# A graph network on one core: gathers ahead of the bulk loads, sort tables in PSUM, twenty tiles written by rows with eighteen norms on GpSimd, and the other tiles' norms earlier in the loop

## Chip, core and metric

One Trainium2 chip, one of its cores. The metric is the device time of one launch in microseconds. The kernel before takes 2309.72 us, the median of three runs (2306.32 to 2310.63).

## What is computed

A graph has 6250 nodes with 16 features and 200000 edges with 16 features each; the edges are sorted by target node `dst`. A learned edge network gives each edge two 16 x 16 matrices (`W_attn`, `W_msg`, with biases); both are multiplied by the source node's features, a softmax over all edges of a target weighs the second by the first, and the sums are added to the node. After a layer norm the mean of the node's edge features is added, and a second layer norm follows:

```python
w_m = (efeat @ W_msg + b_msg).reshape(E, in_f, -1)
w_a = (efeat @ W_attn + b_attn).reshape(E, in_f, -1)
h_src = feat[src][:, :, None]
e1, e2 = w_m * h_src, w_a * h_src
ex = jnp.exp(e2 - segment_max(e2, dst)[dst])
attn = ex / segment_sum(ex, dst)[dst]
ft = segment_sum(e1 * attn, dst).sum(axis=1)
x = layernorm(x + ft)
x = layernorm(x + segment_sum(edge_attr, dst) / max(count, 1))
```

## The kernel before

**Tiles.** Nodes are sorted by degree, on the chip, into NC = 49 tiles of 128 nodes, one node per partition; tile k gets `CAPS[k]` edge slots (56 to 22, falling; 1628 in all), padded to an even number. A slot of a tile is one gather of 128 rows of `xt` by GpSimd (`gather`, L624). Slots go in groups of 8 or 6, and a group is the unit of a step of the loop; there are 224 groups and 240 steps and a few to drain.

**Head (common part).** SP loads constants and then the edge features `ea` in four parts of 3.1 MB (`features`, L458). GpSimd gathers one block of `dst` for each partition (L612), VectorE counts in it where the partition's nodes begin (L1201), GpSimd loads a window of `dst` (`WRUN`, L614) and the first tile's edge rows (L617), then gathers the first 48 slots. VectorE and ScalarE count the window (L1219, L801), which gives each node's degree. VectorE makes a histogram table `OH` of 26 bins x 48 nodes, its running sum `CUM`, ranks, and one-hot tables (`onehot`, L1259) in three sets; TensorE multiplies them (L1007) to permute the nodes. Beside this runs a check that the values stay in a safe range: ScalarE squares `ea` (`squares`, L787; it reads 16 floats apart), TensorE sums them (L993), VectorE takes maxima (L1274), TensorE transposes them (L1003), and VectorE computes `TOT` (L1281 to L1286). All engines wait for `TOT` in `fork` (L405) and take the `regular` branch here. GpSimd then waits for `v_tab`, VectorE's copy of the permuted edge starts `E0I` (L1292), which its next edge-row load needs (`runs_of`, L642).

**Loop.** Per step, TensorE transposes a group of edge features (`T`, L1023), multiplies it by the weights (`W`, L1034, into two pairs of PSUM banks), and adds up the slots of an older group (`gsum`, L1048, 2 matmul records for a slot). VectorE limits the gathered features of a tile once all have landed (`floors`, L1334), multiplies and takes the maximum (`mult`, L1348), multiplies exponentials (`gm`, L1361), and closes a tile (`weigh`, L1378 to L1380). ScalarE moves transposes out of PSUM (L819) and takes the exponentials (L881, L883, L887). The order on each engine is written out by hand from the list `STEPS`. The products lie in a ring of `RING = 66` slots in SBUF, the gathered features in one of 112 slots. After the gathers of tile k GpSimd scatters the result of tile k - 5 to `y_d` in node order (`results`, L657).

**End.** `MAIN = NC - 3 = 46` tiles go through `y_d`: when all have landed (and three scatters of zeros, L678, for the others' rows) SP loads `xt` and `y_d` in node order (L480, L481), VectorE does both layer norms for all 49 x 128 nodes at once, in four pieces `norms(0)` to `norms(3)` (L1402) at steps 235 to 238, and SP writes `out`. The last three tiles have their own `xt` rows gathered (L675); VectorE normalizes them by `last` (L1430, two tiles, then one, with ScalarE's square root at L835), and GpSimd scatters them straight into `out` (L685) after SP's write.

Of the kernel before, what the change touches and what calls it, by code (L numbers as in the profile page):

```python
# [54 lines left out]
MAIN = NC - 3  # L55
# [31 lines left out]
RING = 66  # L87
# [50 lines left out]
NST = len(STEPS) + 4  # L138


def gnn_kernel(nc, xt, dst, src, ea, es, wc, cst, cst2, out):
# [14 lines left out]
    with ctx:  # L156
# [9 lines left out]
        def arena(lowest=0):  # L166
# [50 lines left out]
        DGC = prep([128, RK1])  # L217
        PK = prep([128, RK1])
# [147 lines left out]
        RCL = sb("RCL", [128, 4])  # L366
# [4 lines left out]
        PMB = PX[:, 0, :]  # L371
        PDN = PX[:, 1:3, :].rearrange("p b e -> p (b e)")
# [9 lines left out]
            g_m g_b d_sc d_x a_sq p_sq p_c p_v v_nrm a_x a_p a_out d_y d_yl d_xg v_ys d_ou""".split()  # L382
# [67 lines left out]
        def _(sp):  # L450
# [7 lines left out]
            def features(q):  # L458
                n = min(QE, EC - QE * q)
                sp.dma_start(EAL[:, q % 2, 0:16 * n], ea.rearrange("(p c) w -> p (c w)", p=128)[:, 16 * QE * q:16 * QE * q + 16 * n])\  # L460
                  .then_inc(d_ea[q % 2], 16)

            features(0)
            sp.wait_ge(d_xe[0], 16)
# [13 lines left out]
            def regular():  # L478
                sp.wait_ge(S["d_y"], 16 * NC)
# [8 lines left out]
                sp.wait_ge(S["d_ou"], 48)  # L488
# [107 lines left out]
        def _(g):  # L596
# [11 lines left out]
            g.memset(RAW[:, :], 0.0).then_inc(S["g_m"], 1)  # L608

# [3 lines left out]
            g.wait_ge(S["v_e0"], 1)  # L613
# [17 lines left out]
            def regular():  # L631
# [1214 lines left out]
```

## Time and profile before

| | |
|---|---|
| median of 3 runs | 2309.72 us |
| profiled execution, its time | 2309.43 us |
| its span, first to last instruction | 2307.6 us |
| granted TensorE clock, mean | 0.946 |
| TensorE busy | 2005.4 us (87%) |
| VectorE busy | 1867.7 us (81%) |
| GpSimd busy | 1682.1 us (73%) |
| ScalarE busy | 1306.8 us (57%) |

PE is TensorE, DVE is VectorE, ACT is ScalarE, POOL is GpSimd, SP is the DMA-issuing engine. A line such as `L624` names the line of the kernel; all times are us unless marked ns. An "issue" wait is time in which the engine waited for nothing that the profile shows.

### The profile page before, as it was taken

To read this page: it belongs to the slowest core of one execution; us is meant where nothing else is said; L and a number is where in the kernel's file an instruction comes from. 1 tells how busy PE (TensorE), PEld (TensorE's weight loads), DVE (VectorE), ACT (ScalarE), POOL (GpSimd) and SP (SyncE) were. 2 spreads that over 40 slices of the span, in tenths; PEclk is the share of its full clock that TensorE was granted. 3 is DMA by queue.
4 is the path that set the end of the run, shared out by engine and by line. 5 is a ranking of instruction groups with operands and counts; after the bars stand their busy time and mean duration, and the time that the engine had idled before them with its cause. 6 is when DMAs were issued, how large, how long until landed. Compare 5 with 4: busy or idle time off the path is not lost.

```text
span 2307.6 us, 21909 instructions
## 1 busy us (share of the span) xinstructions
PE 2005.4 (87%) x6784; PEld 911.8 (40%) x6784; DVE 1867.7 (81%) x2922; ACT 1306.8 (57%) x1241; POOL 1682.1 (73%) x1748
## 2 busy tenths in 40 slices
PE   2548889998999998899989898899989898998886
PEld 0313334443444444444444443344444443444432
DVE  5557777987888988888987887798878887888886
ACT  6425545655566556665655755565556565565552
POOL 5777777777777777777777777777777777777740
PEclk8758999999999999999999999999999999999998
DMA  6100011001100001000100110101001010110110
GB/s 232 55 13 13 13 15 19 7 13 18 13 12 13 13 13 17 12 12 13 17 12 12 17 12 12 17 12 16 12 12 16 12 15 12 15 15 11 14 27 9
DMA packets 60072, 46.93 MB, mean 20 GB/s; under 512 B 28526, under 2 KB 55679, under 8 KB 59436
## 3 DMA queue, kind: packets, MB, share of 16 engines
q0 software_dynamic: 57776, 29.87, 9.3%
q1 hardware_dynamic: 2172, 15.58, 1.9%
q8 instruction: 57, 0.93, 0.2%
q14 instruction: 67, 0.55, 0.1%
HBM read 44.01 MB, written 1.23 MB: 20 GB/s over the span
## 4 chain that ended last, share of the span: by engine, by line
PE 36%; POOL 30%; issue 14%; DVE 14%; DMA 2%; ACT 2%; POOLq 0%; DVEq 0%; SPq 0%; ACTq 0%
POOL AR L624 29%; PE PX L1048 28%; PE PW L1034 7%; DVE AR L1348 7%; DVE AR L1361 3%; PE PTB L1023 2%; DVE AR L1378 1%; DMA AR<-in_xt,AR 1%; POOL AR L642 1%; DVE AR L1365 1%; POOL y_d L657 1%; DMA AR<-in_dst,QI 1%; ACT PX L881 0%; DVE AR L1379 0%; DMA AR<-in_es,AR 0%
## 5 line engine op out<-in xcount | busy, mean ns | idle before, releaser
L624 POOL DMA_INDIRECT AR<-in_xt,AR x1628 | 1572.2, 966 | 501.0 <-issue 486.6
L1048 PE MATMUL PX<-AR,CS 128*128 128x512 f32 x3304 | 1583.4, 604 | 6.8 <-ACT AR L825 6.6
L1348 DVE CUSTOM_DVE_ANT_1 AR<-PW,AR 128x1024 f32<-128x1024 f32 x826 | 987.7, 1220 | 183.0 <-PE PW L1034 127.6
L1048 PEld LDWEIGHTS PX<-AR,CS 128*128 128x128 f32 x3304 | 633.7, 193 | 586.5 <-issue 462.6
L1034 PE MATMUL PW<-WS,LT 100*128 100x512 bf16 x1652 | 514.8, 398 | 204.0 <-DVE AR L1348 203.0
L1361 DVE TENSOR_TENSOR AR<-AR,PX 128x1024 f32<-128x1024 f32 (+1 forms) x448 | 508.2, 1134 | 74.3 <-ACT PX L881 47.7
L819 ACT ACTIVATE LT<-PTB 100x1024 bf16<-100x1024 bf16 (+1 forms) x224 | 214.3, 957 | 529.8 <-PE PTB L1023 529.8
L883 ACT ACTIVATE AR<-AR 128x2048 f32<-128x2048 f32 (+1 forms) x224 | 429.3, 1917 | 7.3
L887 ACT ACTIVATE PX<-AR 128x1024 f32<-128x1024 f32 (+1 forms) x224 | 217.2, 970 | 326.4 <-DVE AR L1361 323.6
L1034 PEld LDWEIGHTS PW<-WS,LT 100*128 100x128 bf16 x1652 | 144.9, 99 | 584.2 <-issue 290.0
L881 ACT ACTIVATE PX<-AR 128x1024 f32<-128x1024 f32 (+1 forms) x224 | 235.6, 1052 | 22.9 <-DVE AR L1361 21.3
L1023 PEld LDWEIGHTS PTB<-IDB,AR 128*100 128x100 bf16 x1652 | 126.3, 128 | 132.6 <-issue 118.2
L1023 PE MATMUL PTB<-IDB,AR 128*100 128x128 bf16 x1652 | 132.8, 223 | 13.5 <-POOL AR L662 12.2
L1334 DVE TENSOR_TENSOR AR<-AR 128x128 f32<-128x128 f32 (+13 forms) x68 | 37.4, 563 | 113.6 <-DMA AR<-in_xt,AR 113.1
L1378 DVE RECIPROCAL AR<-AR 128x256 f32<-128x256 f32 x49 | 85.5, 1745 | 0.1
L1348 DVE DVE_READ_ACCUMULATOR2_ANT AR<- 128x1 f32 x826 | 68.4, 83 | 0.0
L825 ACT ACTIVATE AR<-PX 128x512 f32<-128x512 f32 x49 | 29.1, 594 | 52.2 <-PE PX L1048 52.2
L657 POOL DMA_INDIRECT y_d<-AR x46 | 45.0, 977 | 18.4 <-issue 13.4
L642 POOL DMA_INDIRECT AR<-in_es,AR x48 | 46.6, 971 | 14.6 <-issue 10.7
L851 ACT ACTIVATE AR<-AR 128x1088 bf16<-128x1088 bf16 (+13 forms) x49 | 55.6, 1134 | 0.0
L859 ACT ACTIVATE AR<-AR 128x1088 bf16<-128x1088 bf16 (+13 forms) x49 | 54.8, 1119 | 0.0
L1365 DVE TENSOR_REDUCE AR<-AR 128x16 f32<-128x544 f32 (+13 forms) x49 | 53.1, 1084 | 0.0
(149 smaller groups left out, 481.8 us busy)
## 6 DMA issues: line engine op xcount, KB each, us to landing
AR<-in_xt,AR POOLq DMA_INDIRECT x1631, 2.3
AR<-in_ea SPq DMA_DIRECT2D x3, 3128.0 KB, 13.6
AR<-in_ea SPq DMA_DIRECT2D x1, 3120.0 KB, 10.2
AR<-in_es,AR POOLq DMA_INDIRECT x49, 3.5
y_d<-AR POOLq DMA_INDIRECT x49, 2.1
AR<-y_d SPq DMA_DIRECT2D x1, 784.0 KB, 4.6
CS<-in_cst SPq DMA_DIRECT2D x1, 442.0 KB, 5.1
AR<-in_xt SPq DMA_DIRECT2D x1, 392.0 KB, 3.1
```

Of the source, the lines that this page charges most:

```text
L624: g.indirect_dma_start(feat(h, j - j0, j - j0 + 1), None, xt, bass.IndirectOffsetOnAxis(ap=XE[:, at:at + 1], axis=0)).then_inc(hg_sem(h), 16)
L819: a.activation(LT[:, g % 3, 0:128 * n], PTB[0:K, 0:128 * n], ACT.Copy).then_inc(S["a_T"], 1)
L881: a.activation(half(w), x[:, 0:w, :], ACT.Exp, bias=shift).then_inc(S["a_x"], 1)
L883: a.activation(x, x, ACT.Exp, bias=shift).then_inc(S["a_exp"], 1)
L887: a.activation(half(w), x[:, w:2 * w, :], ACT.Copy).then_inc(S["a_x"], 1)
L1023: i = pe.transpose(PTB[0:K, 128 * j:128 * j + 128], part(k, 0, K)[:, j0 + j, :], IDB[:, :])
L1034: i = pe.matmul(PAIRS[s % 2][:, j, :], LT[:, g % 3, lo:lo + 128], WS[:, :], start=True, stop=True)
L1048: i = pe.matmul(PDR, IDN, x, start=(a == 0 and j == 0), stop=(g == LAST[k] and j == n - 1))
L1348: v.tensor_tensor_reduce(em(g, j, j + 2).rearrange("p (x c) -> p x c", c=32), w, hb, 1.0, LOW, ALU.mult, ALU.max, accum_out=MXC[:, k % 2, ...
L1361: v.tensor_tensor(y, y, EXP[:, 0:16 * w].rearrange("p (x o) -> p x o", o=16), ALU.mult).then_inc(S["v_gm"], 1)
L1365: v.tensor_reduce(OUTR[:, k, 16:32], edge(k).rearrange("p j i -> p i j"), AX.X, ALU.add).then_inc(S["v_sa"], 1)
L1378: link(v.reciprocal(RRT, d[:, 0:256]))
```

## The change

1. **Loads.** SP holds `features(0)` until the first tile's edge rows are in; before it SP writes 784 KB of zeros over `y_d` (from `OUTR`, which GpSimd clears at the start), and `features(1)` waits for that write. GpSimd issues the edge rows before `WRUN`. `ea` is read from a transposed copy `eat` that holds each part with the 16 features outermost, so ScalarE's squares read adjacent floats; `squares(0)` comes after ScalarE's counts.
2. **Tables.** `OH`, `DGC`, `QFR`, `KF`, `PK`, a copy `FE1` of the edge starts, and `BASE` lie in PSUM (banks of `PW`), not in SBUF; the running sum takes a constant as its second input. The third one-hot set comes before the maxima. TensorE does the histogram first, then check(0) to check(2), the three permutation sets, check(3) and the transposes. VectorE, not GpSimd, sets the ones of `XP`.
3. **Tiles.** `MAIN` is 29: 20 tiles are written by rows. Of these, 18 get both norms on GpSimd after its last gather, in a batch of 16 and one of 2; the last 2 are normalized by VectorE and ScalarE (`last_batch`). GpSimd's norm has 26 instructions, each waiting for the one before, with a bit-trick root; the means take one more and each batch two additions: 109 in all. Each batch waits for its tiles' results (`a_out`), the first also for `v_ln`. The scatters of zeros and those of tiles 29 to 45 to `y_d` go; 17 more gathers of `xt` come, and 17 more scatters to `out`.
4. **Norms of the other 29 tiles**, still over all nodes at once: 14 pieces `main(0)` to `main(13)`, one a step, at steps 177 to 190 (during tiles 33 to 36).
5. **Last groups.** For the four groups consumed in the last steps without a product (`ADDS`: 218, 221, 222, 223) VectorE adds slots of the second half in pairs (`pairs`), and `gsum` takes 6, 6, 6 and 5 slots in place of 8, 8, 8 and 6.
6. `RING` is 64, which leaves the list of steps as it is; `YN` has its own place.

The diff, cut:

```diff
-MAIN = NC - 3
+MAIN = NC - 20
+REST = NC - MAIN
+BATCH = [(0, REST - 4), (REST - 4, REST - 2), (REST - 2, REST)]
-RING = 66
+RING = 64
+NORMS = [p for p, c in STEPS].index(FIRST[MAIN + 4] + 2)
+ADDS = [c for p, c in STEPS[-8:] if p is None]
...
+        OH = PWF[:, 512:512 + HB * RK1].rearrange("p (b c) -> p b c", c=RK1)
+        DGC, QFR, KF, PK, FE1 = (PWF[:, 1760 + RK1 * x:1760 + RK1 * x + RK1] for x in range(5))
+        BASE = PWF[:, 2000:2000 + HB]
...
+            sp.wait_ge(d_xe[0], 16)
+            sp.wait_ge(S["g_m"], 9)
+            sp.dma_start(YD.rearrange("(p c) w -> p c w", c=NC), OUTR[:, :, :]).then_inc(S["d_yz"], 16)
             features(0)
-            sp.wait_ge(d_xe[0], 16)
+            sp.wait_ge(S["d_yz"], 16)
             features(1)
...
             g.wait_ge(S["v_e0"], 1)
+            g.indirect_dma_start(XE[:, 0:17 * DEG[0]], None, es, bass.IndirectOffsetOnAxis(ap=R0[:, 0:1], axis=0)).then_inc(d_xe[0], 16)
+            g.wait_ge(S["v_e0"], 2)
             g.indirect_dma_start(WRUN[:, :], None, dst.unsqueeze(1), bass.IndirectOffsetOnAxis(ap=RI[:, 0:1], axis=0))\
              .then_inc(S["d_wr"], 16)
...
                 for k in range(1, NC):
                     feats(k)
-                    if k >= 5:
+                    if 5 <= k < MAIN + 5:
                         results(k - 5)
...
                 for k in range(MAIN, NC):
-                    g.indirect_dma_start(XG[:, k - MAIN, :], None, xt, bass.IndirectOffsetOnAxis(ap=NODE[:, k:k + 1], axis=0))\
+                    g.indirect_dma_start(YS[:, k - MAIN, :], None, xt, bass.IndirectOffsetOnAxis(ap=NODE[:, k:k + 1], axis=0))\
                      .then_inc(S["d_xg"], 16)
...
+                def norm(lo, hi):
+                    y, q = YS[:, lo:hi, :], SQS[:, lo:hi, :]
+                    s0, s1, s2 = STS[:, 0, lo:hi], STS[:, 1, lo:hi], STS[:, 2, lo:hi]
+
+                    def row_sums(z):
+                        then(g.tensor_tensor(q[:, :, 0:8], z[:, :, 0:8], z[:, :, 8:16], ALU.add))
+                        then(g.tensor_tensor(q[:, :, 0:4], q[:, :, 0:4], q[:, :, 4:8], ALU.add))
+                        then(g.tensor_tensor(q[:, :, 0:2], q[:, :, 0:2], q[:, :, 2:4], ALU.add))
+                        then(g.tensor_tensor(s0, q[:, :, 0], q[:, :, 1], ALU.add))
+
+                    row_sums(y)
+                    then(g.tensor_scalar(s0, s0, -1.0 / 16, None, ALU.mult))
+                    then(g.tensor_tensor(y, y, s0.unsqueeze(2).broadcast_to([128, hi - lo, 16]), ALU.add))
+                    then(g.tensor_tensor(q, y, y, ALU.mult))
+                    row_sums(q)
+                    then(g.tensor_scalar(s1, s0, 1.0 / 16, 1.0e-5, ALU.mult, ALU.add))
+                    then(g.tensor_scalar(SSI[:, 2, lo:hi], SSI[:, 1, lo:hi], -0.5, 1597463007.0, ALU.mult, ALU.add))
+                    for _ in range(3):
+                        then(g.tensor_tensor(s0, s2, s2, ALU.mult))
+                        then(g.tensor_tensor(s0, s0, s1, ALU.mult))
+                        then(g.tensor_scalar(s0, s0, -0.5, 1.5, ALU.mult, ALU.add))
+                        then(g.tensor_tensor(s2, s0, s2, ALU.mult))
+                    then(g.tensor_tensor(y, y, s2.unsqueeze(2).broadcast_to([128, hi - lo, 16]), ALU.mult))
...
+                g.wait_ge(S["v_ln"], 1)
+                means = OUTR[:, MAIN:NC - 2, 16:32]
+                then(g.tensor_tensor(means, means, RCL[:, 0:REST - 2].unsqueeze(2).broadcast_to([128, REST - 2, 16]), ALU.mult))
+                for b, (lo, hi) in enumerate(BATCH):
+                    if hi < REST:
+                        g.wait_ge(S["a_out"], MAIN + hi)
+                        then(g.tensor_tensor(YS[:, lo:hi, :], YS[:, lo:hi, :], OUTR[:, MAIN + lo:MAIN + hi, 0:16], ALU.add))
+                        norm(lo, hi)
+                        then(g.tensor_tensor(YS[:, lo:hi, :], YS[:, lo:hi, :], means[:, lo:hi, :], ALU.add))
+                        norm(lo, hi)
+                    else:
+                        g.wait_ge(S["v_ys"], 1)
+                    if b == 0:
+                        g.wait_ge(S["d_out"], 48)
+                    for x in range(lo, hi):
+                        g.indirect_dma_start(out, bass.IndirectOffsetOnAxis(ap=NODE[:, MAIN + x:MAIN + x + 1], axis=0), YS[:, x, :], None)\
+                         .then_inc(S["d_ou"], 16)
...
-                a.activation(SQ[:, q % 2, :, 0:n], EAL[:, q % 2, 0:16 * n].rearrange("p (e w) -> p w e", w=16), ACT.Square)\
+                a.activation(SQ[:, q % 2, :, 0:n], EAL[:, q % 2, 0:16 * n].rearrange("p (w e) -> p w e", w=16), ACT.Square)\
...
+            pe.wait_ge(S["v_hist"], 1)
+            pe.matmul(PMB[:, 0:HB], TRI, CNTB[:, :], start=True, stop=True)
+            pe.matmul(PMB[:, HB:2 * HB], ONES[:, :], CNTB[:, :], start=True, stop=True).then_inc(S["p_hist"], 1)
+            check(0)
+            pe.wait_ge(S["v_hist"], 2)
+            check(1)
+            check(2)
+            perm(0)
+            perm(1)
+            perm(2).then_inc(S["p_perm"], 1)
+            check(3)
+            pe.wait_ge(S["v_nrm"], 1)
...
+                def pairs(g):
+                    half = GRP[g][2] // 2
+                    keep = KEPT(half)
+                    v.wait_ge(S["a_exp"], g + 1)
+                    v.wait_ge(S["v_gm"], 2 * g + 2)
+                    sums = em(g, half, 2 * half - keep)
+                    v.tensor_tensor(sums, sums, em(g, half + keep, 2 * half), ALU.add).then_inc(S["v_ad"], 1)
...
-                    if 0 <= i - USED[LAST[MAIN]] - 2 < 4:
-                        norms(i - USED[LAST[MAIN]] - 2)
-                    if i - 3 == USED[LAST[NC - 2]]:
-                        last(0, 2)
-                last(2, 3)
+                    if 0 <= i - NORMS < 14:
+                        main(i - NORMS)
+                last_batch()
```

## Rows read from the trace of the kernel before

**Rows 1.** The page, part 1: busy time, share of the span, instructions.
```profile
PE 2005.4 (87%) x6784; PEld 911.8 (40%) x6784; DVE 1867.7 (81%) x2922; ACT 1306.8 (57%) x1241; POOL 1682.1 (73%) x1748
```
**Rows 2.** The page, part 5: group, busy us, mean ns, idle before and its releaser.
```profile
L624 POOL DMA_INDIRECT AR<-in_xt,AR x1628 | 1572.2, 966 | 501.0 <-issue 486.6
```
**Rows 3.** Who waited for whom: us in total, times, longest us.
```profile
DVE AR L1334 <- DMA AR<-in_xt,AR: 113.1, 27, 26.1
```
**Rows 4.** Timeline of VectorE, L1334: start us, us, instruction, idle before and releaser.
```profile
1132.43 0.72 DVE L1334 TENSOR_TENSOR AR<-AR 128x544 f32<-128x544 f32 x1 [2.31 <-DMA AR<-in_xt,AR]
...
1761.43 0.66 DVE L1334 TENSOR_TENSOR AR<-AR 128x480 f32<-128x480 f32 x1 [5.41 <-DMA AR<-in_xt,AR]
```
**Rows 5.** Busy time by stretch: stretch, its length, engines, clock, DMA share, GB/s.
```profile
1630.00:2230.00 600.00, 546.50 (x1845) 248.25 (x1844) 504.45 (x796) 352.28 (x356) 452.56 (x474) 0.97 0.10 13
```
**Rows 6.** Timeline of GpSimd in the head.
```profile
9.55 1.11 POOL L612 DMA_INDIRECT AR<-in_dst,QI  x1 [3.09 <-DVE QI L1196]
23.89 1.22 POOL L614 DMA_INDIRECT AR<-in_dst,AR  x1 [13.22 <-DVE AR L1204]
...
31.83 0.95 POOL L624 DMA_INDIRECT AR<-in_xt,AR  x1 [5.47 <-DMA AR<-in_es,AR]
...
45.58 2.02 POOL L624 DMA_INDIRECT AR<-in_xt,AR  x1 [0.30 <-issue]
...
102.96 0.95 POOL L642 DMA_INDIRECT AR<-in_es,AR  x1 [0.30 <-issue]
```
**Rows 7.** Timeline of VectorE in the head.
```profile
22.48 0.75 DVE L1201 TENSOR_SCALAR_CACHE_REDUCE AR<-AR,CS 128x512 f32<-128x512 f32 x1 [12.15 <-DMA AR<-in_dst,QI]
...
29.59 0.30 DVE L1219 TENSOR_SCALAR_CACHE_REDUCE AR<-AR,CS 128x88 f32<-128x88 f32 x1 [3.83 <-DMA AR<-in_dst,AR]
...
45.32 1.46 DVE L1227 TENSOR_TENSOR AR<-AR,CS 128x1248 f32<-128x1248 f32 x1
...
69.21 1.50 DVE L1274 TENSOR_REDUCE NRM<-PW 128x1 f32<-128x391 f32 x3
...
92.33 0.21 DVE L1292 CAST AR<-PX 128x49 int32<-128x49 f32 x1 [2.03 <-PE PX L1007]
```
**Rows 8.** DMA issues: what, engine, count, KB each, median us to landing.
```profile
AR<-in_xt,AR POOLq DMA_INDIRECT x1631, 2.3
AR<-in_ea SPq DMA_DIRECT2D x3, 3128.0 KB, 13.6
...
AR<-in_es,AR POOLq DMA_INDIRECT x49, 3.5
```
**Rows 9.** Timeline of ScalarE in the head.
```profile
13.90 0.87 ACT L786 ACTIVATE AR<-AR 125x800 f32<-125x800 f32 x1 [2.40 <-DMA AR<-in_xt]
22.29 10.73 ACT L792 ACTIVATE AR<-AR 128x6256 bf16<-128x6256 f32 x1 [7.52 <-DMA AR<-in_ea]
```
**Rows 10.** Groups by line: TensorE's permutation.
```profile
L1007 PE MATMUL PX<-AR 128*128 128x98 f32 x96 | 11.1, 276 | 0.0
```
**Rows 11.** Timeline of GpSimd in the tail.
```profile
2216.83 0.98 POOL L657 DMA_INDIRECT y_d<-AR  x1 [0.30 <-issue]
...
2295.51 0.96 POOL L685 DMA_INDIRECT out<-AR  x1 [3.85 <-DVE AR L1445]
```
**Rows 12.** Timeline of VectorE in the tail: a wide and a small operation.
```profile
2243.88 0.98 DVE L1408 TENSOR_TENSOR AR<-AR 128x784 f32<-128x784 f32 x1
...
2258.90 0.21 DVE L1395 TENSOR_TENSOR AR<-AR 128x49 f32<-128x49 f32 x1
```
**Rows 13.** Timeline of TensorE in the tail.
```profile
2249.20 0.60 PE L1034 MATMUL PW<-WS,LT 100*128 100x512 bf16 x2 [3.29 <-DVE AR L1348]
...
2267.04 19.26 PE L1048 MATMUL PX<-AR,CS 128*128 128x512 f32 x44 [1.73 <-ACT AR L825]
```
**Rows 14.** Timeline of GpSimd at the start.
```profile
0.74 0.51 POOL L597 MEMSET AR<- 1x512 bf16 x1 [0.29 <-POOLq L1836]
1.31 0.30 POOL L600 MEMSET AR<- 1x256 bf16 x1
```

More of the change, by code:

```diff
@@ L676, in regular @@
                      .then_inc(S["d_xg"], 16)
-                for k in range(MAIN, NC):
-                    g.indirect_dma_start(YD, bass.IndirectOffsetOnAxis(ap=NODE[:, k:k + 1], axis=0), OUTR[:, 0, :], None)\
-                     .then_inc(S["d_y"], 16)
-                for k in range(NC - 5, MAIN):
-                    results(k)
-                g.wait_ge(S["d_out"], 48)
-                for k in range(MAIN, NC):
-                    g.wait_ge(S["v_ys"], 1 if k < NC - 1 else 2)
-                    g.indirect_dma_start(out, bass.IndirectOffsetOnAxis(ap=NODE[:, k:k + 1], axis=0), YS[:, k - MAIN, :], None)\
-                     .then_inc(S["d_ou"], 16)
+                done = [0]
@@ new lines, in then @@
+                def then(i):
+                    done[0] += 1
+                    i.then_inc(S["g_b"], 1)
+                    g.wait_ge(S["g_b"], done[0])
+                def norm(lo, hi):
[19 more added lines that the diff above has]
+                    then(g.tensor_tensor(y, y, s2.unsqueeze(2).broadcast_to([128, hi - lo, 16]), ALU.mult))
@@ L808, in _ @@
             counts(0, len(BY_ACT))
+            squares(0)
             squares(1)
@@ L988, in _, with check @@
             pe.wait_ge(S["v_id"], 1)
-            for q in range(NQE):
+            def check(q):
                 n = min(QE, EC - QE * q)
@@ L1271, in _ @@
             onehot(*CUTS[1])
+            onehot(*CUTS[2])
             for q in range(NQE):
@@ L1408, in norms @@
                         link(v.tensor_tensor(XNN, XNN, YN[:, :, 0:16], ALU.add))
[L1409 to L1413 removed]
+                    if 1 <= x < 6:
+                        norm(x - 1)
+                    if x == 6:
+                        link(norm(5))
                         link(v.tensor_tensor(YN[:, :, 16:32], YN[:, :, 16:32], wide(RCG), ALU.mult))
+                    if x == 7:
@@ new lines, in added, with last_batch @@
+                def added(lo, hi):
+                    link(v.tensor_tensor(YS[:, lo:hi, :], YS[:, lo:hi, :], OUTR[:, MAIN + lo:MAIN + hi, 16:32], ALU.add))
+                def last_batch():
+                    lo, hi = BATCH[2]
+                    st = STS[:, :, lo:hi]
+                    for x in range(2):
+                        centre(lo, hi)
+                        spread(SQS[:, lo:hi, :], st).then_inc(S["v_var"], 1)
+                        v.wait_ge(S["a_z"], x + 1)
+                        link(v.reciprocal(STS[:, 0, lo:hi], STS[:, 2, lo:hi]))
+                        i = v.tensor_tensor(YS[:, lo:hi, :], YS[:, lo:hi, :], wide(STS[:, 0, lo:hi]), ALU.mult)
+                        if x == 0:
+                            link(i)
+                            added(lo, hi)
+                    i.then_inc(S["v_ys"], 1)
@@ L1465, in regular @@
                         gm(c, 1)
+                        if c in ADDS:
+                            pairs(c)
                     if nx is not None:
@@ L1802 @@
     eap = np.concatenate([ea, np.zeros((EP - E, 16), ea.dtype)])
+    eat = np.concatenate([eap.reshape(128, EC, 16)[:, lo:lo + EC // NQE + 1].transpose(0, 2, 1).reshape(128, -1)
+                          for lo in range(0, EC, EC // NQE + 1)], 1)
     srcp = np.concatenate([src, np.zeros(EP - E, src.dtype)])
```

211 lines of the change are left out of this document (96 added, 115 removed).

## The prediction

> **What bounds the kernel now.** I read the page first. GpSimd counts as busy for 73% of the span [rows 1], which looks harmless; the costliest groups show otherwise. The 1628 feature gathers of L624 take 0.966 us each, and in front of each stands 0.30 us of issue and nothing else [rows 2]. So GpSimd issues one DMA every 1.25 us, 1628 x 1.266 = 2061 us of a 2307.6 us span, with 48 loads of `in_es` and 46 scatters at the same price in the same queue. The only other place where the loop runs dry is VectorE waiting for gathered features, 113.1 us in 27 waits [rows 3]. In the timeline the longest, 26.1, stands before the first whole tile; then there is none until tile 20 at 1132 (2.31), and from there on almost each tile has one of 1 to 6 us, such as 5.41 at tile 35 [rows 4]. Thus GpSimd sets the start of the loop, TensorE and VectorE pace tiles 2 to 19 at nearly the same rate, and GpSimd sets the pace again from tile 20. There TensorE is busy 546.5 of 600 us and VectorE 504.5 [rows 5]: GpSimd may become some 5% faster before TensorE holds the loop.
>
> Three stretches are therefore worth money: the time to GpSimd's first gather, what stands in its queue, and the tail after its last gather.
>
> **Head: first gather.** The gather of `in_dst` by QI is issued at 9.55 and VectorE can use it only at 22.48, because the first 3.1 MB of `in_ea` were put in ahead of it [rows 6, 7]. In the change SP holds `features(0)` until the first edge rows are in. An indirect load of 487 KB lands in 3.5 us in the loop [rows 8]; this one is half as large, I take 3.3, so VectorE starts at 12.9, 9.6 earlier. The edge rows are then issued first, not second behind a slot of 1.5 us (1.22 + 0.30 at L614), at 14.4; with 3.5 us to land and 0.7 to start, the first L624 is at 18.6 instead of 31.83: 13.2 us. Bounds: 10 if the two loads take as long as before relative to each other, 14 at best.
>
> **Head: table stalls.** From 31.83 to L642 at 102.96 stand 48 gathers, 71.1 us where 48 x 1.25 = 60 would do. The 11.1 too many are in long issues such as 2.02 us at 45.58, beside VectorE's L1227 at 45.32 [rows 6, 7]. These are its tensor operations with both inputs in SBUF. The change puts one input of each (OH, QFR, KF, PK, FE1, BASE) into PSUM. The Trainium skill, "SBUF — State Buffer", section on the shared port pair, says that a VectorE instruction with two SBUF inputs contends with a GpSimd one that reads SBUF; the trace agrees so far. I take all 11.1; at worst nothing, but see what is late next. GpSimd would be at the fork (L642) at 18.6 + 60 = 78.6, and the two memsets of XP that leave its queue give 0.4.
>
> **Head: what is late next.** GpSimd goes on only when VectorE has copied E0I (L1292, 92.33) [rows 7]. Before, that was 10 us early; now it decides. The working: the long WRUN load lands about 22.5 (issued 15.7, 5.6 us before, more beside YD's zeroing, 0.8 MB, and `features(0)`). From the first count to the first L1274 VectorE took 69.21 - 29.59 = 39.6 us [rows 7], so with the third one-hot set it is done by about 67. The four squares: a load of `in_ea` takes 13.6 us [rows 8]. The first lands about 34, the second 44.5; the third can be issued only after `squares(0)`, and lands about 54.5. `squares` took 10.73 us for 6256 elements, 1.7 ns each, reading every 16th float, while L786 took 0.87 for 800, 1.1 ns with all its fixed time [rows 9]; with the transposed `eat` I take 5.9. Third squares done at 60.5, check(2) on PE to 65, then 48 permutation pairs, 11.1 us [rows 10], to 76. check(3), now behind them, ends at 80.5, for the maxima, the transposes and the verdict I put 3.5, for fork and copy 1.3 (these two, with the end of the permutation between them, are the last of the stretch to 92.33): E0I at 85.3. So GpSimd waits 6.7 us at the fork, and L642 moves from 102.96 to about 85.7. With the 0.4 of the memsets the **head gains 17.5 us**; the ends are 10.5 (E0I no earlier than now) and 24.8 (no wait). All consumers follow, since the first whole tile starts when its gathers land.
>
> **Loop.** Scatters to `y_d` cost 0.98 + 0.30 [rows 11]. Those of tiles 29 to 42, 14 of them, no longer stand before the last gather: -17.9. The two layer norms over all nodes go from the last steps to 177 to 190 (tiles 33 to 36). They are 13 wide operations of 1.01 us and 22 small of 0.24, with reciprocals 19.3 us [rows 12]. Per tile 4 to 6 us, what VectorE waits there (5.41 at tile 35 [rows 4]): I cost them at nothing on the end; without that cover up to 10 us. Their two-input forms will hold up some gathers: +3. SP's loads of XNN and YN wait for the result of tile 28 and have some 20 us until step 177. The other queues lose nothing.
>
> **Tail, TensorE and VectorE.** The norms no longer stand between the last multiplications. TensorE sat 3.3 us for VectorE at 2246 and 1.73 at 2265.3, and then did 22 slots in 19.26, 0.87 each [rows 13]. `pairs` adds slots of the last groups on VectorE, so 7 slots fall away: 6.1. Together 11.1. The last batch has two tiles for one, +0.3, and one more scatter, +1.25: this path ends 9.6 earlier, beside the head's gain.
>
> **Tail, GpSimd.** Today it idles there; now it won't. Without the head's gain: the slot after the last gather is at 2216.83 [rows 11], -17.9 + 3 = 2201.9. Twenty gathers of `xt`, 25.0, and landing 2.3 [rows 8]: 2229.2. Then 109 dependent small instructions over some 4200 elements per partition. No row shows such arithmetic on GpSimd. Lower bound 0.22, VectorE's small operation [rows 12]; upper bound 0.57, from the first memset to the one that waits for it (0.74 to 1.31); that second takes 0.30 by itself [rows 14]. I take 0.28, nearest the single memset, and VectorE's 1.25 ns per element: 109 x 0.28 + 5.3 = 35.8 (29 to 67). Sixteen scatters 20.3, two more 2.5, then the last two 1.6: the last one starts at 2289.4, against 2295.51 [rows 11]. So **the tail gains 6.1**, by GpSimd's chain, not by the 9.6 of the other path.
>
> The Trainium skill, "GPSIMD Engine Reference", section 3, speaks against this part: elementwise work on GpSimd is about 2x slower, 4497 ns for 2048 elements with two inputs. At that price an estimate for the 4200 elements is 9.2 us, not 5.3, and the tail would gain 2.
>
> **Sum.** 2309.43 (span 2307.6 and 1.8 around it, 0.3 below the median of the runs) - 17.5 - 6.1 = 2285.8.
>
> **Rivals.**
> A, the forecast: 0.45, between 2278 and 2296.
> B, full cover: E0I comes before 78.6, and GpSimd's norms cost 0.25 or less, so that the other path ends last: 2309.4 - 24.8 - 9.6 = 2275. For: VectorE has its tables at 67. Against: permutations wait behind the third squares. 0.2.
> C, slower: GpSimd's arithmetic is the new end. At 0.57 each the chain is 31.6 longer: 2285.8 + 31.6 = 2317. It decides from 0.49 each (23.6 / 109 more than 0.28). For: 109 instructions in series, each with a wait. Against: the memsets' own 0.3. 0.12.
> D, the head's new wait takes more: the loads of `in_ea` start 13 us later and all four are behind one another, so E0I stays at 92.5: 2309.4 - 10.5 - 6.1 = 2293. 0.13.
> E, the moved norms aren't hidden, since TensorE has only 9% left there: 10 us late at the last tile, the path of TensorE ends 0.4 later than before: 2309.4 - 17.5 + 0.4 = 2292. 0.1.
>
> **Numbers.** The likeliest is A, 2286. The range 2270 to 2308 holds B, D and E with their bounds and leaves out C. 0.2% (4.6 us) is about what a measurement can tell from no change. Faster: A, B, most of D and E, 0.85; same, 0.05, from the upper part of D and E; slower, 0.1, C.
>
> **What would show it.** First L624 near 18.6. Forty-eight gathers in 60 us without long issues. A gap of some 7 us on GpSimd before L642, ended by VectorE's copy. Squares of 5.9 us each. Waits at tiles 35 to 46 shorter by about 1 us each. In the tail, GpSimd's small instructions 0.28 us apart, and its last scatter waiting for none of VectorE's (rival B: for VectorE's last norm). I am wrong if the small instructions are 0.5 apart, or if L642 stays after 95.

## The result, and the profile of the changed kernel

The change takes 2276.62 us, the median of 4 runs (2275.09 to 2278.06), against 2308.02 for the kernel before (4 runs, 2305.4 to 2310.63: the three of its table and one more): ratio 0.9864, 95% interval 0.9847 to 0.9881. It is faster by 31.4 us; the forecast was 2286.0, a gain of 23.4 on the profiled execution. The profiled execution of the change took 2275.09, with a span of 2273.2. The median lies within the whole range, 2270 to 2308, but 1.4 below the 2278 to 2296 that the prediction gave to its own case A.

The page, parts 1 and 5, answers to [rows 1] and [rows 2]; the third line is from the list of who waited for whom and answers to [rows 3].

```profile
PE 1984.3 (87%) x6770; PEld 903.9 (40%) x6770; DVE 1868.7 (82%) x2907; ACT 1295.0 (57%) x1240; POOL 1711.5 (75%) x1870
...
L634 POOL DMA_INDIRECT AR<-in_xt,AR x1628 | 1556.3, 956 | 498.5 <-issue 485.5
```
```profile
DVE AR L1394 <- DMA AR<-in_xt,AR: 67.9, 20, 19.7
```

GpSimd's 1628 gathers still have nothing but the 0.30 of issue in front of them; they take 15.9 us less in sum (1572.2 before), and VectorE waits 45.2 us less for them (113.1 before). The engine that paces the kernel is the same one.

GpSimd's timeline in the head, against [rows 6]:

```profile
9.86 1.13 POOL L622 DMA_INDIRECT AR<-in_dst,QI  x1 [2.09 <-DVE QI L1252]
14.73 1.22 POOL L624 DMA_INDIRECT AR<-in_es,AR  x1 [3.74 <-DVE AR L1260]
16.25 0.95 POOL L626 DMA_INDIRECT AR<-in_dst,AR  x1 [0.30 <-issue]
19.84 0.94 POOL L634 DMA_INDIRECT AR<-in_xt,AR  x1 [2.65 <-DMA AR<-in_es,AR]
...
78.50 0.94 POOL L634 DMA_INDIRECT AR<-in_xt,AR  x1 [0.30 <-issue]
81.06 0.94 POOL L652 DMA_INDIRECT AR<-in_es,AR  x1 [1.61 <-DVE AR L1350]
```

The first gather starts at 19.84 instead of 31.83, 48 gathers take 47 x 1.248 from first to last, so none of them is long, and the fork's gather of edge rows (L652, L642 before) starts at 81.06 instead of 102.96: 21.9 us earlier. In front of it stand 1.61 us, 1.31 more than a mere issue.

What those 1.31 wait for is E0I, copied by VectorE in L1350. ScalarE's squares, TensorE and VectorE in the same stretch, against [rows 9], [rows 10] and the last row of [rows 7]:

```profile
35.59 5.41 ACT L837 ACTIVATE AR<-AR 128x6256 bf16<-128x6256 f32 x1
...
52.91 5.42 ACT L837 ACTIVATE AR<-AR 128x6256 bf16<-128x6256 f32 x1 [4.71 <-DMA AR<-in_eat]
```
```profile
58.39 4.29 PE L1034 MATMUL PW<-AR,IDB 128*128 128x391 bf16 x16 [3.12 <-ACT AR L837]
62.51 10.86 PE L1040 MATMUL PX<-AR 128*128 128x98 f32 x96
73.21 2.80 PE L1034 MATMUL PW<-AR,IDB 128*128 128x390 bf16 x16
```
```profile
68.69 1.50 DVE L1333 TENSOR_REDUCE NRM<-PW 128x1 f32<-128x391 f32 x3
76.05 0.56 DVE L1333 TENSOR_REDUCE NRM<-PW 128x1 f32<-128x390 f32 x1 [5.86 <-PE PW L1034]
...
80.36 0.21 DVE L1350 CAST AR<-PX 128x49 int32<-128x49 f32 x1 [0.72 <-DVE TOT L1344]
```

The chain is the one of the prediction: load, squares, check(2), permutations, check(3), verdict, copy. It ends 5 us sooner than forecast.

GpSimd in the tail, against [rows 11]: its slot after the last gather (the first L680), the first instructions of the norms, two long ones, the first scatter, the second batch's begin, and the last scatters.

```profile
2171.94 0.95 POOL L680 DMA_INDIRECT CS<-in_xt,AR  x1 [0.30 <-issue]
...
2198.58 0.74 POOL L717 TENSOR_TENSOR AR<-AR,RCL 128x288 f32<-128x288 f32 x1 [1.36 <-DMA CS<-in_xt,AR]
...
2204.11 0.32 POOL L695 TENSOR_TENSOR AR<-AR 128x64 f32<-128x64 f32 x1
...
2205.74 0.22 POOL L707 TENSOR_TENSOR AR<-AR 128x16 f32<-128x16 f32 x1
2206.04 0.22 POOL L708 TENSOR_TENSOR AR<-AR 128x16 f32<-128x16 f32 x1
...
2211.42 1.37 POOL L695 TENSOR_TENSOR AR<-AR 128x64 f32<-128x64 f32 x1
...
2221.03 1.49 POOL L711 TENSOR_TENSOR CS<-CS,AR 128x256 f32<-128x256 f32 x1
2222.80 1.08 POOL L730 DMA_INDIRECT out<-CS,AR  x1 [0.28 <-POOL CS L711]
...
2243.32 0.26 POOL L721 TENSOR_TENSOR CS<-CS,AR 128x32 f32<-128x32 f32 x1
...
2258.96 1.05 POOL L730 DMA_INDIRECT out<-CS,AR  x1 [0.28 <-POOL CS L711]
...
2262.84 0.96 POOL L730 DMA_INDIRECT out<-CS,AR  x1 [0.30 <-issue]
```

TensorE's last products (against [rows 13]) and VectorE's last multiplication of its own two tiles:

```profile
2215.27 15.00 PE L1104 MATMUL PX<-AR,CS 128*128 128x512 f32 x34 [0.69 <-ACT AR L870]
```
```profile
2237.65 0.19 DVE L1521 TENSOR_TENSOR CS<-CS,AR 128x32 f32<-128x32 f32 x1
```

VectorE is done at 2237.8, when GpSimd has yet to issue the first batch's last four scatters, to do the second batch, and to scatter four more tiles. GpSimd's chain sets the end, by 25 us.

**Where the 34.3 us of the two profiled executions (2309.43 - 2275.09) come from.** The slot after the last gather is 44.9 us earlier (2216.83 to 2171.94): 21.9 from the head, 0.4 from the two memsets of XP that stood behind the fork (from the fork's gather to the next one it was 1.65 us, now 1.25), 17.9 from 14 scatters, and 4.7 are left for the loop, where fewer gathers were long (the gathers' sum fell by 15.9, of which 11.2 in the head). From that slot to the last scatter it is 90.9 us instead of 78.7: 12.2 lost. From the last scatter to the end 12.25 instead of 13.92: 1.7 gained, with no instruction in that stretch in either trace.

### The profile page after: what moved, and what is told of

It reads as the page before. It is cut to its first block, busy times and chain, and to the rows that moved or that the text cites. A ratio compares the mean times of both kernels' runs of the same rounds, so it can differ in the third digit from the quotient of the medians.

```text
span 2273.2 us, 21991 instructions
## 1 busy us (share of the span) xinstructions
PE 1984.3 (87%) x6770; PEld 903.9 (40%) x6770; DVE 1868.7 (82%) x2907; ACT 1295.0 (57%) x1240; POOL 1711.5 (75%) x1870
## 4 chain that ended last, share of the span: by engine, by line
PE 47%; POOL 21%; DVE 14%; issue 12%; DMA 3%; ACT 3%; POOLq 0%; DVEq 0%; SPq 0%; ACTq 0%
PE PX L1104 36%; POOL AR L634 17%; PE PW L1084 9%; DVE AR L1408 7%; DVE AR L1421 3%; PE PTB L1073 2%; DVE AR L1440 1%; DMA AR<-in_xt,AR 1%; POOL CS L680 1%; POOL out L730 1%; DVE AR L1433 1%; DMA AR<-in_eat 1%; ACT AR L846 0%; DVE AR L1377 0%; ACT PX L920 0%
## 5 line engine op out<-in xcount | busy, mean ns | idle before, releaser
L634 POOL DMA_INDIRECT AR<-in_xt,AR x1628 | 1556.3, 956 | 498.5 <-issue 485.5
L922 ACT ACTIVATE AR<-AR 128x2048 f32<-128x2048 f32 (+1 forms) x224 | 436.2, 1947 | 7.3
L1073 PE MATMUL PTB<-IDB,AR 128*100 128x128 bf16 x1652 | 132.2, 222 | 11.9 <-ACT AR L898 10.7
L1394 DVE TENSOR_TENSOR AR<-AR 128x128 f32<-128x128 f32 (+13 forms) x68 | 37.4, 564 | 68.7 <-DMA AR<-in_xt,AR 67.9
L1408 DVE DVE_READ_ACCUMULATOR2_ANT AR<- 128x1 f32 x826 | 67.9, 82 | 0.0
L652 POOL DMA_INDIRECT AR<-in_es,AR x48 | 46.2, 962 | 15.9 <-issue 11.6
L1370 DVE TENSOR_TENSOR AR<-AR 128x544 f32<-128x544 f32 (+13 forms) x49 | 35.7, 728 | 4.5 <-DMA AR<-in_es,AR 2.9
```

The source lines that it names most:

```text
L634: g.indirect_dma_start(feat(h, j - j0, j - j0 + 1), None, xt, bass.IndirectOffsetOnAxis(ap=XE[:, at:at + 1], axis=0)).then_inc(hg_sem(h), 16)
L922: a.activation(x, x, ACT.Exp, bias=shift).then_inc(S["a_exp"], 1)
L1073: i = pe.transpose(PTB[0:K, 128 * j:128 * j + 128], part(k, 0, K)[:, j0 + j, :], IDB[:, :])
L1408: v.tensor_tensor_reduce(em(g, j, j + 2).rearrange("p (x c) -> p x c", c=32), w, hb, 1.0, LOW, ALU.mult, ALU.max, accum_out=MXC[:, k % 2, ...
```

## The experiments

The theory: GpSimd's queue sets the time from its first gather to its last scatter, so an edit is worth what it does to that queue, or to the one result that the queue waits for. The rivals say that TensorE and VectorE hold some part of it. All times are medians of 4 or 5 runs, beside the kernel before on the same chip (2306.29 to 2309.31 in three groups of runs); edits are made in the changed kernel. The change itself was not run again in these groups, and each ratio is good to about 0.0017, so a difference between two kernels is good to some 6 us of time; the smaller ones are read from the traces.

**The tables back in SBUF.**

```diff
-        OH = PWF[:, 512:512 + HB * RK1].rearrange("p (b c) -> p b c", c=RK1)
-        DGC, QFR, KF, PK, FE1 = (PWF[...] for x in range(5))
-        BASE = PWF[:, 2000:2000 + HB]
+        OH = prep([128, HB, RK1])
...
+        FE1 = SS[:, 1:NC]
+        BASE = JK[:, 256:256 + HB]
```

> The changed kernel with its sort tables (OH, DGC, QFR, KF, PK, BASE) back in SBUF and the copy FE1 left out. Theory 1 (GpSimd's queue is the bound from its first gather to its last scatter): the long issues come back among the 48 gathers of the head, 11 us in all, of which the 1.3 us that GpSimd now waits for E0I beyond the usual 0.30 absorb a part; the kernel takes 2276.6 + 9.8 = 2286. Theory 2 (E0I decides the head, the gathers before it have slack): at most 2278.

Measured: 2289.18 (2287.17 to 2294.7), ratio 0.9912 (0.9894 to 0.9930): 12.6 us above the change. GpSimd's timeline of this kernel, two of its long gathers (eleven take over 1.1 us, nine of them over 1.5) and the fork, and VectorE's of the same stretch:

```profile
40.76 1.54 POOL L638 DMA_INDIRECT AR<-in_xt,AR  x1 [0.31 <-issue]
42.60 2.42 POOL L638 DMA_INDIRECT AR<-in_xt,AR  x1 [0.30 <-issue]
...
91.90 0.94 POOL L656 DMA_INDIRECT AR<-in_es,AR  x1 [0.30 <-issue]
```
```profile
40.02 1.46 DVE L1287 TENSOR_TENSOR AR<-AR,CS 128x1248 f32<-128x1248 f32 x1
41.51 2.76 DVE L1290 TENSOR_TENSOR_SCAN AR<-AR,LASTP 128x1248 f32<-128x1248 f32 x1
...
79.76 0.21 DVE L1353 CAST AR<-PX 128x49 int32<-128x49 f32 x1 [0.72 <-DVE TOT L1347]
```

Both long gathers stand beside a VectorE instruction with both inputs in SBUF, and each ends 0.8 us after it: the one from 40.76 at 42.30, after the instruction of 40.02 to 41.48, and the one from 42.60 at 45.02, after the running sum of 41.51 to 44.27. VectorE's own two take 1.46 and 2.76 here and 1.47 and 2.76 in the change, and E0I (79.76) is ready 12 us before GpSimd asks: the stall is on GpSimd's side. The eleven hold 11.2 us too many, the 11.1 of the prediction; the fork is 10.8 later, since the first gather starts 0.9 later here and the 1.3 us of waiting for E0I are gone. The Trainium skill, "SBUF — State Buffer", section "Who interferes with whom", says that a VectorE instruction with two SBUF inputs contends with a GpSimd one that reads SBUF; the trace agrees, with these rows.

**The edge features' first load ahead again.**

```diff
+            features(0)
             sp.wait_ge(d_xe[0], 16)
...
-            features(0)
```

> The changed kernel with the first 3.1 MB of edge features issued at once, as before, and not held until the first tile's edge rows are in; the rest of the order stays. Theory 1: VectorE can use the dst block at 22.5 instead of 13.3, the first gather starts near 29, and the kernel takes 2276.6 + 9 to 11 = 2286 to 2288. Theory 2 (E0I decides, and it may even come earlier as the loads start earlier): within 3 us of 2276.6.

Measured: 2287.48 (2284.03 to 2288.06), ratio 0.9903 (0.9885 to 0.9920): 10.9 above the change. The edge rows are issued at 23.26 and the first gather starts at 28.48, 8.6 later; E0I comes at 87.45, behind counts that start 8.0 later, and the fork's gather at 88.50, 7.4 later than in the change:

```profile
23.26 1.22 POOL L624 DMA_INDIRECT AR<-in_es,AR  x1 [12.59 <-DVE AR L1260]
...
28.48 0.94 POOL L634 DMA_INDIRECT AR<-in_xt,AR  x1 [2.75 <-DMA AR<-in_es,AR]
```

The small gather (L622) is issued at 9.53 here and at 9.86 in the change; with 3.1 MB ahead of it VectorE uses it at 21.85 instead of 13.32, 8.5 us later. Rival D, that putting the bulk loads behind costs the head what it gives, falls: they start later in the change, and E0I is still earlier.

**The squares read every 16th float again.**

```diff
-                sp.dma_start(EAL[...], eat[:, 16 * QE * q:16 * QE * q + 16 * n])\
+                sp.dma_start(EAL[...], ea.rearrange("(p c) w -> p (c w)", p=128)[:, 16 * QE * q:16 * QE * q + 16 * n])\
...
-                ... EAL[:, q % 2, 0:16 * n].rearrange("p (w e) -> p w e", w=16), ACT.Square)\
+                ... EAL[:, q % 2, 0:16 * n].rearrange("p (e w) -> p w e", w=16), ACT.Square)\
```

> The changed kernel with ea read in its old layout, so that ScalarE's squares again read every 16th float. The sums are the same. Squares take 10.7 us each instead of 5.4; the third ends near 68, the permutation behind it near 83.5, the copy E0I comes near 90.6 instead of 80.4. Theory 1: GpSimd waits 10 us more at the fork and the kernel takes 2286 to 2287. Rival (the permutation can start on what it has, or the loads and not the squares set the pace): under 2281.

Measured: 2289.52 (2287.33 to 2292.72), ratio 0.9913 (0.9895 to 0.9931): 12.9 above the change, 2.5 more than the top of what was expected. ScalarE, and GpSimd at the fork:

```profile
36.16 43.04 ACT L837 ACTIVATE AR<-AR 128x6256 bf16<-128x6256 f32 x4
```
```profile
91.74 0.94 POOL L652 DMA_INDIRECT AR<-in_es,AR  x1 [11.17 <-DVE AR L1350]
```

Four squares take 43.04 back to back, 10.76 each, and E0I comes at 91.05. The fork's gather is 10.7 later; another 2 us of the median come from elsewhere, and the length of the loop differs by some us from kernel to kernel (below).

So three edits, each undone alone, move the fork's gather by 10.8, 7.4 and 10.7 us, of the 21.9 that the head gained. Their times stand 12.6, 10.9 and 12.9 above the change; by the ratios to the kernel before (0.9912, 0.9903 and 0.9913 against 0.9864) it is 11, 9 and 11. The three shifts don't add up to the whole, because the fork's gather waits for the later of two chains: GpSimd's own 48 gathers (done for the next at 78.5 + 1.25) and the squares with E0I (80.36). The tables lengthen the first alone, the strided squares the second alone, the early load both: 8.6 us on the gathers, 7.1 on E0I, whose permutations then wait for VectorE's tables.

**The fifteen scatters put back, to a spare tensor.** The tiles from the thirtieth on, but the last five, are also scattered in the loop, as the kernel before did; the output doesn't use it.

```diff
+                    if k >= MAIN + 5:
+                        g.wait_ge(S["a_out"], k - 4)
+                        g.wait_ge(S["v_sa"], k - 4)
+                        g.indirect_dma_start(ZD, ...NODE[:, k - 5:k - 4, ]..., OUTR[:, k - 5, :], None)
```

> The changed kernel with the dropped scatters of results put back at their places in GpSimd's queue, for tiles 29 to 43, into a spare DRAM tensor that nobody reads: 14 before the last gather and one behind it, 1.28 us each. Theory 1 (GpSimd's queue, end to end): 15 x 1.28 = 19.2 us, so 2276.6 + 19.2 = 2296. Rival (by tiles 34 to 48 GpSimd is held up by the ring or by the consumers, so that a slot in its queue is free): under 2285.

Measured: 2298.34 (2296.99 to 2299.19), ratio 0.9961 (0.9947 to 0.9976): 21.7 above the change, 2.5 more than 15 x 1.28 = 19.2. The slot after the last gather is at 2196.73, 24.8 later than in the change; the gathers sum to 1561.6, 5.3 more than the change's 1556.3, and the rest is the scatters. What GpSimd no longer issues is worth its full price.

**The other tiles' norms left out.** The pieces 1 to 6 and 8 to 13 do nothing: centring, squares, sums, roots and scaling of the first 29 tiles are left out.

```diff
-                    if 1 <= x < 6:
-                        norm(x - 1)
...
-                        link(norm(5))
...
-                    if 8 <= x < 13:
-                        norm(x - 8)
```

> The changed kernel without the centring, squares, sums, inverse roots and scaling of the norms of the first 29 tiles, some 15 us of VectorE in steps 177 to 190; the additions, the means' product and the loads and writes stay. Theory 1: GpSimd's chain does not depend on them beyond a few longer issues, so the time is 2273 to 2277; and TensorE's end moves by less than 5 us, since the pieces stand where VectorE waited for gathers. Rival (the norms in the loop cost the consumers their full length): TensorE's last product ends 10 to 15 us earlier than 2230, measured against the slot after the last gather (58.3 us behind it in the changed kernel).

Measured: 2275.5 (2275.08 to 2278.94), ratio 0.9867 (0.9850 to 0.9883): 1.1 below the change, which can't be told from nothing. The waits of L1394 for gathered features, tiles 38 and 39, in this kernel and then in the change:

```profile
1846.03 0.66 DVE L1394 TENSOR_TENSOR AR<-AR 128x448 f32<-128x448 f32 x1 [2.82 <-DMA AR<-in_xt,AR]
1882.48 0.66 DVE L1394 TENSOR_TENSOR AR<-AR 128x448 f32<-128x448 f32 x1 [5.31 <-DMA AR<-in_xt,AR]
```
```profile
1847.70 0.62 DVE L1394 TENSOR_TENSOR AR<-AR 128x448 f32<-128x448 f32 x1
1880.82 0.62 DVE L1394 TENSOR_TENSOR AR<-AR 128x448 f32<-128x448 f32 x1
```

From 1690 to 1890, the stretch of the norms, the waits of that kind sum to 19.5 us without them and to 2.8 with them: 16.7 more. VectorE's busy time is 13.4 lower (1855.3 against 1868.7), for this edit leaves out the two norms but keeps the additions and the means' product among the 19.3 us of the pieces. So the norms run in the time in which VectorE would have waited. (Over the whole loop the sums are 87.7 and 67.9; in the other kernels that have these norms in the loop they are 67.0 to 83.9, so the totals alone would show nothing.) TensorE's last product ends 60.2 us behind GpSimd's slot after the last gather, 58.3 in the change: not 10 to 15 us earlier, as the rival had it.

**The same norms 16 steps later, and in the last 16 steps.**

```diff
-NORMS = [p for p, c in STEPS].index(FIRST[MAIN + 4] + 2)
+NORMS = [p for p, c in STEPS].index(FIRST[MAIN + 4] + 2) + 16
```
```diff
+NORMS = NST - 16
```

> The fourteen pieces of the layer norms of the first 29 tiles stand 16 steps later in the loop than in the change (tiles 37 to 40 instead of 33 to 36), nothing else differs. Theory 1 (GpSimd's queue bounds from the first gather to the last scatter, and these norms fill VectorE's waits for features wherever such waits are): they still end before GpSimd's slot after the last gather (near 2172), the waits at tiles 33 to 36 stay, those at 40 to 43 (2.8 and 4.1 in the change) shrink, and the time is that of the change: 2276.6, plus or minus 2. Theory 2 (the norms cost where the loop is bound by VectorE and TensorE, and their place decides): 2280 or more, or under 2273.

> The same fourteen pieces stand in the last 16 steps of the loop, as the kernel before has them in its last ones; nothing else differs from the change. Theory 1: GpSimd's first batch of norms waits for them (its results are scattered over those of the store of all nodes), so it starts near 2235 instead of 2198.6, when the last piece is done on VectorE, and the chain behind it keeps its length: 35 to 45 us longer, 2312 to 2322, so slower than the kernel before. Theory 2 (where these norms stand matters little, since GpSimd's chain has slack or can overlap them): within 10 us of the change, under 2287.

Measured: 2278.42 (2277.2 to 2278.48), ratio 0.9865 (0.9848 to 0.9881), for the first: as the change (0.9847 to 0.9881). There the waits at tiles 34 to 38 are 5.35, 2.87, 3.99, 2.99 and 3.32 us (in the change 1.76, 1.08 and then none), and those at tiles 40 and 41, 2.77 and 4.08 in the change, are gone, as expected. For the second 2319.04 (2315.79 to 2319.94), ratio 1.0039 (1.0025 to 1.0053): 42.4 above the change and slower than the kernel before. GpSimd after its 20 gathers, in the second:

```profile
2199.94 0.94 POOL L680 DMA_INDIRECT CS<-in_xt,AR  x1 [0.31 <-issue]
2244.86 0.67 POOL L717 TENSOR_TENSOR AR<-AR,RCL 128x288 f32<-128x288 f32 x1 [43.98 <-DVE AR L1471]
```

It sits 43.98 us for the last piece of VectorE's norms, and only then starts its own chain, 62 us to the last scatter. So the last piece may end anywhere before 2198; behind that it is paid for, here 46 us later for 42 us of time. Moving the norms is thus no gain of its own, but with them in the last steps the twenty tiles by rows, and all the rest, give nothing.

**Last groups without pairs.**

```diff
-ADDS = [c for p, c in STEPS[-8:] if p is None]
+ADDS = []
```

> The changed kernel with VectorE's pair sums of the last groups undone, so TensorE adds 7 slots more. Theory 1: TensorE's last product ends 6 us later, but GpSimd's last scatter stands 25 us behind VectorE's last norm, so the time stays at 2276.6, within 2. Rival (TensorE's end decides): 2282.

Measured: 2277.07 (2275.81 to 2278.8), ratio 0.9872 (0.9856 to 0.9889). TensorE's last run of products is again 19.33 for 44 records instead of 15.00 for 34, and it ends at 2239.9, still 23 us before the last scatter (2263.49). Nothing of the 4.3 us reaches the end. The additions have a price in the change: both long instructions of the norms shown above, 1.37 at 2211.42 and 1.49 at 2221.03, stand beside them. In this kernel, without the additions, the same two take 0.33 and 0.62: 1.9 us less, and the first batch takes 22.2 us instead of 23.9. That too is too little to be seen in the medians, 0.5 apart. The additions in the change, and then the two instructions here:

```profile
2211.39 1.23 DVE L1429 TENSOR_TENSOR AR<-AR 128x1024 f32<-128x1024 f32 x1
...
2220.81 1.23 DVE L1429 TENSOR_TENSOR AR<-AR 128x1024 f32<-128x1024 f32 x1
```
```profile
2214.29 0.33 POOL L695 TENSOR_TENSOR AR<-AR 128x64 f32<-128x64 f32 x1
...
2222.88 0.62 POOL L711 TENSOR_TENSOR CS<-CS,AR 128x256 f32<-128x256 f32 x1
```

**Four tiles for VectorE, sixteen for GpSimd.** GpSimd's second batch goes to the engines that are done 25 us before.

```diff
-BATCH = [(0, REST - 4), (REST - 4, REST - 2), (REST - 2, REST)]
+BATCH = [(0, REST - 4), (REST - 4, REST)]
...
+                        v.wait_ge(S["a_out"], NC - 2)
+                        two = YS[:, REST - 4:REST - 2, :]
+                        link(v.tensor_tensor(two, two, OUTR[:, NC - 4:NC - 2, 0:16], ALU.add))
```

> The changed kernel with the second batch of two tiles taken from GpSimd; VectorE and ScalarE normalize the last four tiles at once instead of two. Theory 1: GpSimd's chain ends last in the tail, by 23 us over VectorE's last norm (2237.8 against a last scatter at 2262.8), so the 54 small instructions, 15.4 us, come off the end: 2276.6 - 15.5 = 2261. Rival (VectorE and TensorE decide the end): no change or a little slower, 2276 to 2278.

Measured: 2261.69 (2261.49 to 2263.96), ratio 0.9796 (0.9778 to 0.9813): 14.9 below the change, against 15.4 for the batch that is gone. It is the fastest kernel of this study (the next one can't be told from it) and beats both the kernel before and the change. GpSimd goes from scatter to scatter:

```profile
2227.26 1.08 POOL L730 DMA_INDIRECT out<-CS,AR  x1 [0.28 <-POOL CS L711]
...
2251.81 0.95 POOL L730 DMA_INDIRECT out<-CS,AR  x1 [0.30 <-issue]
```
```profile
2244.99 0.23 DVE L1524 TENSOR_TENSOR CS<-CS,AR 128x64 f32<-128x64 f32 x1
```

VectorE's last multiplication ends at 2245.2, before GpSimd comes to its four tiles.

**And 33 tiles through `y_d`.** On top of that, four tiles fewer by rows.

```diff
-MAIN = NC - 20
+MAIN = NC - 16
```

> The kernel with four tiles on VectorE, and 16 tiles by rows instead of 20 (12 normalized by GpSimd, 33 tiles through y_d). GpSimd's queue loses 4 gathers of xt and 4 scatters to out in the tail and gets 4 scatters to y_d: 5 us less. VectorE's last norm stands only 2.8 us before the scatter that waits for it in the kernel before this one, so 2.5 to 3 us come off: 2261.7 - 2.5 = 2259. If the norms, now four tiles later, cost the consumers something: 2262 to 2266.

Measured: 2262.25 (2261.26 to 2267.59), ratio 0.9811 (0.9794 to 0.9828). The expected 2.5 us less didn't come. GpSimd's last four scatters:

```profile
2247.65 0.96 POOL L730 DMA_INDIRECT out<-CS,AR  x1 [9.15 <-DVE CS L1524]
...
2251.44 0.96 POOL L730 DMA_INDIRECT out<-CS,AR  x1 [0.30 <-issue]
```

GpSimd is through with its twelve tiles and waits 9.15 us for VectorE's last multiplication (2247.14 to 2247.4). The end has passed to the other path. That path begins with the last gather, and the four additional scatters stand ahead of it: the slot behind it is at 2180.14 instead of 2177.28, TensorE's last products start at 2224.40 instead of 2222.24. Between 16 and 20 tiles by rows there should thus be a point where both chains end together; no run tried it, and with the last scatter at 2251.4 and 2251.8 on either side it has little to give.

## Why the prediction was right, and by how much its terms were off

The mechanism was right in each part that sets the time, and the sizes were not: by the profiled executions the forecast gain was 23.4 and the measured 34.3, 10.9 too small (9.4 by the medians).

**Head, first gather and table stalls: right.** First gather 18.6 forecast, 19.84 measured: the block of `dst` was usable 3.5 after its issue, as said, but from the issue of the edge rows to the first gather it was 5.1, not 4.2. All 11.1 us of stalls went, and they came back with the tables.

**Head, what is late next: mechanism right, term too large.** E0I was put at 85.3 and came at 80.36; GpSimd waits 1.3 for it, not 6.7. The squares took 5.41, not 5.9; the third was done at 58.3, not 60.5. check(3) with its 16 records took 2.80, not 4.4, so it ended 2.6 behind the permutations, where 4.5 were added. With the first gather the head gained 21.9 where 17.1 was put, without memsets. (The prediction's own terms, from 102.96 to 85.7, add up to 17.3, and 17.7 with the memsets, not 17.5.)

**Loop: the scatters right, the rest smaller than the traces can tell.** 14 scatters went at full price (shown with 15). The norms were hidden as said: leaving them out gives 1.1 us, moving them by 16 steps nothing; rival E falls. The waits at tiles 35 to 46 were to be 1 us shorter each and were 2 (46 us in sum before, 20 in the change). The step "their two-input forms will hold up some gathers: +3" stands 7.7 off against the profiled execution, where the loop was 4.7 shorter than the sum without it. But that can't be put down to the change. From the fork's gather to the slot after the last gather the change took 2090.9; six kernels with the same work there (tables in SBUF, first load ahead, strided squares, no pairs, four tiles on VectorE, norms 16 steps later) took 2095.3 to 2099.4, and the one without norms 2093.6. The prediction's own sum gives 2095.6 without the +3 and 2098.6 with it. So the loop of the change's profiled execution was some 5 us shorter than its like, though the median of its four runs is only 1.5 above it; no run shows why. Whether the norms' two-input forms cost those 3 us of gathers stays open.

**Tail, GpSimd: mechanism right, one price too low.** It sets the end, as forecast. The slot-to-last-scatter stretch was put at 87.5 and took 90.9. The arithmetic was put at 35.8 and took 39.3 (23.9 for the first batch, 15.4 for the second). The two batches give its terms: 54 instructions with some 436 elements take 15.4; 55 with some 3776 take 23.9, or 22.0 without the 1.9 beside the pairs (22.2 in the kernel without pairs). That is 0.27 us an instruction and 1.9 ns per element. The 0.28 was right (rival C falls; its bound, 0.28 + 23.6 / 109, is 0.50). The 1.25 ns of VectorE failed: GpSimd takes half as much again, and 1.9 us more went where VectorE's pairs stood beside. The Trainium skill's price ("GPSIMD Engine Reference", section 3) gave 9.2 us for the elements, an estimate, against 4212 x 1.9 ns = 8.0 by these two batches and 5.3 put. The trace agrees with the page that GpSimd is the slower one for elementwise work, and its price was nearer than mine.

**Tail, TensorE and VectorE: a term left out.** This path was to end 17.5 + 9.6 = 27.1 earlier. It ended 57.4 earlier: VectorE's last multiplication at 2237.8, in the kernel before at 2295.2:

```profile
2295.05 0.18 DVE L1445 TENSOR_TENSOR AR<-AR 128x16 f32<-128x16 f32 x1
```

Counted from the slot after the last gather it gained 12.5 (78.4 to 65.9), near the 9.6. What the sum forgot is the loop: the 14.9 of the scatters and norms were given to GpSimd's chain alone, though by the prediction GpSimd paces the other two from tile 20 on. With them its own numbers put 18 us between the two ends, not 3.5; measured are 25. That cost the forecast nothing, for this path was the earlier one, but it hid the room in which four tiles on VectorE gained 15 us. And it makes rival B's 2275, which the measured 2276.6 lies nearer to than A's 2286, a coincidence: B's sum lacks the same 14.9, and neither of its conditions came true, for E0I came after 78.6 (80.36) and GpSimd's last scatter waited for nothing of VectorE's.

**The end.** From the last scatter to the end the change took 1.7 less. In the ten kernels of the experiments it is 11.5 to 12.3 too; no run shows why.

Sum of the misses: 12.5 at the slot (4.8 head with the memsets, 7.7 loop), less 3.4 in the chain, plus 1.7 at the end: 10.8.

**By parts**, each as its own undoing shows it: tables 12.6, order of loads 10.9, squares 12.9 (these three share the head's 22), fifteen scatters 21.7, pairs nothing, norms of the other tiles nothing by themselves but needed. What was left to gain was the second batch of two tiles on GpSimd: 54 instructions for 2 of 49 tiles cost 15.4 us on the path, while VectorE with four tiles ends 8.0 us after TensorE's last product instead of 7.6 with two.

## What to carry to other kernels

When one engine's queue paces a kernel, price an edit by what it adds to or takes from that queue, and check where the engine goes idle afterwards: work may move to where another engine waits at no cost, as the norms did here, 13.4 us of busy time, but only until the first point at which the pacing engine needs its result. A chain of dependent small instructions costs mostly by their count, so a batch of 2 tiles costs two thirds of what a batch of 16 does (15.4 against 23.9 us); join batches, and hand the small one to the engine that is already done. If the undoings of several edits of one stretch add up to more than the gain of all (here 10.8, 7.4 and 10.7 of 21.9), look for a place where two chains meet.

## What the runs showed of the hardware

- GpSimd arithmetic where each instruction waits for the one before: the starts are 0.28 us apart for 2 to 8 elements, 0.30 for 16, 0.32 to 0.35 for 32, 0.70 to 0.81 for 256 with two inputs; by the two batches it is 0.27 us for each instruction and 1.9 ns per element.
- Such arithmetic is held up by VectorE in the same way as gathers are: the same instruction over 64 elements took 1.37 us beside VectorE's pair addition and 0.33 in the kernel without it.
- VectorE's running sum with two SBUF inputs holds up a gather too (2.42 instead of 0.94); with one input of each in PSUM none of 48 gathers was long (0.94 or 0.95 each).
- ScalarE took 5.41 us for 6256 adjacent floats and 10.76 for the same number 16 floats apart.
- TensorE did the same 16 records of L1034 in 4.29 us at 58.39 and in 2.80 at 73.21. The granted clock was 0.64 in the first stretch and 1.00, the level of 2.4 GHz, in the second. Before the first TensorE had stood idle for 3.12 us; before the second it had done the permutations for 10.86 us without a gap:

```profile
58.39:62.60 4.21, 4.21 (x18) 2.22 (x18) 4.18 (x4) 1.91 (x1) 3.15 (x4) 0.64 0.17 38
...
73.21:76.01 2.80, 2.80 (x18) 1.47 (x16) 0.00 (x0) 0.00 (x0) 1.89 (x3) 1.00 0.07 6
```

  (Columns: stretch, its length, busy time of TensorE, weight loads, VectorE, ScalarE, GpSimd, clock, DMA share, GB/s.) In the kernel before, check(3) took 4.37 after 6.05 idle; the 1.6 us between the two are part of what the chain that ends in E0I gained, and the prediction had not counted them; no run moved check(3) alone. Idle time just before is not the whole of it: in the change check(1), the same 16 records at 52.45, took 2.83 at a granted clock of 1.00 though TensorE had stood idle for 3.28 us before it, and check(0) at 45.02 took 4.15 at a clock shown as 1.00. What decides is not shown here.
